# Projecting the queries of a pair of heads first: order q, k, k, q for k, k, q, q in two fused attention stages

## The reference

```python
x = x + attn_a(layernorm(x))   # q, k, v from x; 16 heads of 64; softmax(q k^T / (64*64*16)) v; WO
x = x + ffn(layernorm(x))      # gelu(x w1 + b1) w2 + b2, 256 -> 1024 -> 256
x = x + attn_b(layernorm(x))   # layernorm again, down to 128, up to q, k, v; RoPE on q and k; 1/sqrt(64)
x = x + ffn(layernorm(x))
```

## Time and profile before

| | before |
|---|---|
| median of 3 runs | 3870.42 us (3868.67 to 3873.36) |
| the profiled execution, its own time | 3868.46 us |
| its span | 3866.7 us |
| mean granted clock of TensorE, as a share of full speed | 0.978 |
| PE busy | 3650.3 us, 94% |
| POOL busy | 2624.3 us, 68% |
| PEld busy | 2354.9 us, 61% |
| DVE busy | 2262.3 us, 59% |
| ACT busy | 1689.1 us, 44% |
| DMA queue q1 (SP's) | 291.48 MB, 38.2% of 16 engines' span |

### The profile page before, as it was taken

One profiled execution on the slowest core, in us unless ns is written; L12 is line 12 of the kernel. 1 busy time (PEld: TensorE's weight loads), 2 busy tenths in 40 slices (PEclk: granted clock), 3 DMA queues, 4 the chain that ended last, 5 costly groups with the idle time before them and its releaser, 6 DMA issues. The chain is left out here.

```text
span 3866.7 us, 60118 instructions
## 1 busy us (share of the span) xinstructions
PE 3650.3 (94%) x16736; PEld 2354.9 (61%) x16736; DVE 2262.3 (59%) x2988; ACT 1689.1 (44%) x3212; POOL 2624.3 (68%) x1467
## 2 busy tenths in 40 slices
PE   3999999999999999997975999999999999999799
PEld 2566666666666666656863555555555555555488
DVE  5444444444444444445756777777777767777354
ACT  1344444444444444444542444444444444444354
POOL 2677777778777777773323777887788778777521
PEclk9999999999999999998996999999999999999899
DMA  6334433343344434421114455445544454554100
GB/s 194 81 80 88 103 78 75 84 109 84 81 85 87 95 75 86 87 47 32 44 62 90 80 86 103 83 84 86 103 83 84 83 105 82 85 83 83 40 17 28
DMA packets 419601, 313.68 MB, mean 81 GB/s; under 512 B 254753, under 2 KB 292513, under 8 KB 418465
## 3 DMA queue, kind: packets, MB, share of 16 engines
q1 hardware_dynamic: 414400, 291.48, 38.2%
q10 hardware_dynamic: 5088, 20.97, 1.5%
HBM read 88.35 MB, written 21.50 MB: 28 GB/s over the span
## 5 line engine op out<-in xcount | busy, mean ns | idle before, releaser
L887 POOL TENSOR_TENSOR a_rs<-a_rs,a_p 128x1024 f32<-128x1024 f32 x384 | 916.0, 2385 | 317.9 <-ACT a_p L797 301.0
L814 DVE TENSOR_REDUCE a_nmax<-a_ps_x 128x1 fp32r<-128x1024 f32 x512 | 627.2, 1225 | 759.4 <-PE a_ps_x L620 755.8
L887 POOL TENSOR_TENSOR b_rs<-b_rs,b_p 128x1024 f32<-128x1024 f32 x384 | 916.8, 2387 | 227.0 <-ACT b_p L797 208.9
L814 DVE TENSOR_REDUCE b_nmax<-b_ps_x 128x1 fp32r<-128x1024 f32 x512 | 626.7, 1224 | 326.5 <-PE b_ps_x L620 322.3
L797 ACT ACTIVATE a_p<-a_ps_s 128x512 f32<-128x512 f32 x1024 | 529.7, 607 | 413.6 <-PE a_ps_s L636 412.8
L797 ACT ACTIVATE b_p<-b_ps_s 128x512 f32<-128x512 f32 x1024 | 530.6, 608 | 340.6 <-PE b_ps_s L636 332.0
L652 PE MATMUL a_ps_o<-a_p,a_v 128*64 128x512 f32 x2048 | 467.7, 598 | 0.0
L652 PE MATMUL b_ps_o<-b_p,b_v 128*64 128x512 f32 x2048 | 467.7, 598 | 0.0
L635 PE MATMUL b_ps_s<-b_q,b_k 128*128 128x512 f32 x1024 | 419.5, 410 | 2.9 <-ACT b_p L797 1.5
L635 PE MATMUL a_ps_s<-a_q,a_k 128*128 128x512 f32 x1024 | 416.2, 406 | 3.0 <-DMA a_q<-a_nmax 3.0
L636 PE MATMUL b_ps_s<-b_q,b_k 128*128 128x512 f32 x1024 | 404.7, 395 | 0.0
(11 more groups left out here) (166 smaller groups left out, 5692.8 us busy)
## 6 DMA issues: line engine op xcount, KB each, us to landing
a_k<-a_nat_h SPq DMA_DIRECT2D x256, 128.0 KB, 2.4
a_q<-a_nat_h SPq DMA_DIRECT2D x256, 128.0 KB, 2.4
b_k<-b_nat_h SPq DMA_DIRECT2D x256, 128.0 KB, 3.9
b_q<-b_nat_h SPq DMA_DIRECT2D x256, 128.0 KB, 3.8
a_k<-a_nat_l SPq DMA_DIRECT2D x128, 128.0 KB, 2.4
a_q<-a_nat_l SPq DMA_DIRECT2D x128, 128.0 KB, 2.4
a_rinv<-rows_a SPq DMA_DIRECT2D x128, 128.0 KB, 3.0
b_k<-b_nat_l SPq DMA_DIRECT2D x128, 128.0 KB, 4.0
```

The source lines that it names most:

```text
L814: dve.reduce_max(nmax[:, g % 2, head, qi:qi + 1], ps_x[:].rearrange("p a b -> p (a b)"), AX_X, negate=True).then_inc(s_red, 1)
L887: pool.tensor_tensor(out, out, p[:, bb, i, :], ALU.add).then_inc(s_sum, 1)
```

## The change

In each pair the projections come as q of half 0, k of half 0, k of half 1, q of half 1. The same four projections are computed in the same places of PE's stream; what each of them is has changed. With it:

- `stack(4p)` is now a stack of q, whose slot is free early, so it moves to the top of the odd window; only `stack(4p + 1)`, k of half 0, stays at its end.
- `stack` and `convert` use buffer n % 2 as before; cosine, sine and feature columns go by the real half.
- q's split weights now serve n % 4 = 0 and 3, and live in two slots (`wq_h`, `wq_l` get a dimension of 2). Loads and splits of q and k swap places: wk in even windows, wq in odd ones.
- The lead-in loads and splits q's weights first.

The diff, cut to its core:

```diff
-        wq_r, wq_h, wq_l = sb("wq_r", [P, WC]), sb("wq_h", [P, WC], F32R), sb("wq_l", [P, WC], F32R)
+        wq_r, wq_h, wq_l = sb("wq_r", [P, WC]), sb("wq_h", [P, 2, WC], F32R), sb("wq_l", [P, 2, WC], F32R)
...
+        def which_half(n):
+
+            return ((1, 0), (0, 0), (0, 1), (1, 1))[n % 4]
...
         def maxima(pe, t, c):
...
-                        pe.wait_ge(s_stack[half], due(t, 2 * SD, SD * (pair + 1)))
-                pe.wait_ge(s_stack[2 + g % 2], due(t, 2 * SD, SD * (pair + 1)))
+                        pe.wait_ge(s_stack[1 + half], due(t, 2 * SD, SD * (pair + 1)))
+                pe.wait_ge(s_stack[3 * (g % 2)], due(t, 2 * SD, SD * (pair + 1)))
...
         def project_qk(pe, t, u, n):
...
+                pe.wait_ge(s_wq, due(t, 4, 2 * (pair + 1)))
+            if n % 4 == 1:
                 pe.wait_ge(s_wk, due(t, 4, 2 * (pair + 1)))
-            if n % 4 == 2:
-                pe.wait_ge(s_wq, due(t, 4, 2 * (pair + 1)))
...
         def pool_window(pool, t, u):
...
-                    split(pool, t, wk_r, wk_h, wk_l, s_wkr, s_unit, due(t, 8, 4 * pair - 2), s_wk, pair, 2)
+                    split(pool, t, wq_r, wq_h[:, pair % 2, :], wq_l[:, pair % 2, :], s_wqr, s_unit,
+                          due(t, 8, 4 * pair - 4), s_wq, pair, 2)
...
-                    split(pool, t, wq_r, wq_h, wq_l, s_wqr, s_unit, due(t, 8, 4 * pair), s_wq, pair, 2)
+                    split(pool, t, wk_r, wk_h[:], wk_l[:], s_wkr, s_unit, due(t, 8, 4 * pair - 1), s_wk, pair, 2)
...
         def sp_window(sp, t, u):
...
-            if u % 2 == 0 and live(t, 8, n, 4 * NPAIR):
+            if live(t, 8, n, 4 * NPAIR):
                 sp.wait_ge(s_nat_l, due(t, 8, n + 1))
                 stack(sp, n)
...
-            if u % 2 == 1 and live(t, 8, n, 4 * NPAIR):
-                stack(sp, n)
+            if u % 2 == 1 and live(t, 8, n + 1, 4 * NPAIR):
                 stack(sp, n + 1)
```

More of the change, by code:

```diff
@@ L684, in project_qk @@
         def project_qk(pe, t, u, n):
-            pair, which, half = n // 4, (n % 4) // 2, n % 2
+            pair = n // 4
+            which, half = which_half(n)
             if n % 4 == 0:
                 pe.wait_ge(s_feat, due(t, 16, 16 * (pair // 2 + 1)))
+                pe.wait_ge(s_wq, due(t, 4, 2 * (pair + 1)))
+            if n % 4 == 1:
                 pe.wait_ge(s_wk, due(t, 4, 2 * (pair + 1)))
-            if n % 4 == 2:
-                pe.wait_ge(s_wq, due(t, 4, 2 * (pair + 1)))
             pe.wait_ge(s_nat_l, due(t, 8, n))
-            w_h, w_l = (wk_h, wk_l) if which == 0 else (wq_h, wq_l)
+            w_h, w_l = (wk_h, wk_l) if which == 0 else (wq_h[:, pair % 2, :], wq_l[:, pair % 2, :])
             if rope is not None:
@@ L750, in convert_hi @@
         def convert_hi(act, t, n):
-            half, which = n % 2, (n % 4) // 2
+            half, which = n % 2, which_half(n)[0]
             if rope is None:
@@ L817, in rotate_odd @@
         def rotate_odd(dve, t, n):
-            cols = slice((n % 2) * BLOCK, (n % 2 + 1) * BLOCK)
+            half = which_half(n)[1]
+            cols = slice(half * BLOCK, (half + 1) * BLOCK)
             dve.wait_ge(s_unit, due(t, 8, n + 1))
@@ L907, in stack @@
         def stack(sp, n):
-            pair, which, half = n // 4, (n % 4) // 2, n % 2
+            pair = n // 4
+            which, half = which_half(n)
             for head in range(2):
                 rows = slice(D * head, D * (head + 1)) if rope is None else slice(head, P, 2)
-                hi, lo = nat_h[rows, half, :].bitcast(F32), nat_l[rows, half, :].bitcast(F32)
+                hi, lo = nat_h[rows, n % 2, :].bitcast(F32), nat_l[rows, n % 2, :].bitcast(F32)
                 if which == 0:
@@ L967, in sp_window @@
                 source = source_of(t, 3 + u // 2)
-                sp.wait_ge(s_wk, due(t, 4, u + 6))
-                sp.dma_start(wk_r[:], w_qk[source, :, WC:2 * WC]).then_inc(s_wkr, 16)
+                sp.wait_ge(s_wq, due(t, 4, u + 6))
+                sp.dma_start(wq_r[:], w_qk[source, :, 0:WC]).then_inc(s_wqr, 16)
             if u == 2 and live(t, 1, 2, BODIES):
@@ L1024, in _ @@
             pool.memset(q2[0:D, :, :, :].bitcast(F32), 0.0).then_inc(s_init, 1)
-            split(pool, 0, wk_r, wk_h, wk_l, s_wkr, s_unit, 0, s_wk, 0, 2)
+            split(pool, 0, wq_r, wq_h[:, 0, :], wq_l[:, 0, :], s_wqr, s_unit, 0, s_wq, 0, 2)
             pool.memset(ones[:], 1.0).then_inc(s_init, 1)
-            split(pool, -1, wv_r, wv_h, wv_l, s_wvr, s_vp, due(-1, 4, 4), s_wv, 1, 1)
+            split(pool, -1, wv_r, wv_h[:], wv_l[:], s_wvr, s_vp, due(-1, 4, 4), s_wv, 1, 1)
             run(pool, pool_window)
```

12 lines of the change are left out of this document (6 added, 6 removed).

## The result

The changed kernel takes 3847.40 us (median of 6 runs, 3845.88 to 3851.33); the kernel before, run between them, 3870.43. The ratio is 0.9943, with a 95% interval of 0.9932 to 0.9954: 23.0 us faster by the medians, where the sum said 24.1 and the forecast was 3846.

The account below looks back on a forecast made before the run. PE was taken as full in steady state, leaving lead-ins and transfer waits. Terms of 24.1 us took the profiled 3868.5 to 3844.4; against the median before, 3870.4, the forecast was 3846, range 3832 to 3860.

Parts of the forecast that it names:

- lead-in of a: Start of attention a: stack 0 goes once low part 0 is written, first maximum moves from 93.51 to about 89.7, -3.8 us.
- lead-in of b: Start of attention b: earlier stack 0 and no queue backlog move the first maximum from 2068.07 to 2064.0, -4.1 us.
- even windows of b: Steady state of b: ACT's wait for the stack of twelve ends, 0.22 us in 15 bodies, -3.3 us.
- reloads of b: Three feature reloads inside attention b: 3.5 of 6.7 us saved at each, -10.5 us, between -3 and -20.
- reloads of a: Three reloads in a: rinv issued earlier, next group's scores no longer wait 0.77 us for shift DMAs, -2.4 us.
- odd windows: Steady state: rinv's spread goes later, behind six stack DMAs, but POOL's multiply has 3.5 us of cover, cost 0.
- from there on the chain of maxima and reductions is what it was: Attention a after its first maximum: the chain is unchanged and starts earlier, keeping the 3.8 us.
- the first wait: Reload of b: PE's 1.53 us for the last stack DMA before the pair's first maximum goes or shrinks to half a microsecond.
- of 4.0 us idle about 2 stay: Each reload of b: PE's waits for the stack and for POOL's multiply behind rinv together shrink from 4.0 to about 2 us.
- A: Only the lead-ins move; PE idles as long at reloads because rinv still lands after them: 3858 us, chance 0.17.
- B: POOL's multiply in odd windows, behind stack and spread, becomes a bound: half a microsecond each, 3876.4 us, chance 0.04.
- C: Nothing gained: half-clock stretches swallow the lead-in shifts and steady state is PE's, 3866 us, chance 0.08.
- D: At reloads q1 keeps moving or rinv gets through, POOL's multiply is not late, stalls go whole: 3837 us, chance 0.16.

Follow-up runs that it names:

- the last kernel: Changed kernel with rinv ahead of the stack and b's reload halved, k and v's half behind window u=1's first exponential: 3835.83 us, ratio 0.9913.

## Why the prediction was right

The total was right, and the places and the kinds of the gains were right. Two sizes inside the largest term were not, and that the total came out within 1.1 us of the sum is in part luck. Term by term, with the values of the two profiles of the changed kernel:

| term | forecast | measured |
|---|---|---|
| lead-in of a | -3.8 | -2.9, -2.5 at the first maximum; -2.2, -2.2 at the first scores |
| lead-in of b | -4.1 | -4.1, -4.1 at both |
| even windows of b | -3.3 | -1.5 (23.46 to 23.34 us, 12 times without the reloads' own) |
| reloads of b | -10.5 | -4.4, -7.2 in the profiles, -8.2, -7.9 in the two others with these reloads; -9.7 by the medians without reloads |
| reloads of a | -2.4 | -3.0 (25.28, 25.24, 25.35 to 24.33, 24.29, 24.27) |
| odd windows | 0 | 0 (23.25 to 23.26 in b) |
| not in the sum: first body of b | | -1.1, -1.6 |

With 2.3 us for the lead-in of a (below) and 9.7 for the reloads of b these come to some 22 us, with the profiles' 7 to 8 for the reloads to some 20, for 23.0 measured. What fills the gap of 1 to 3 us was not found; the interval of the measurement is wider than that.

*Lead-in of a.* The shape was right, two sizes were not. The stack of projection 0 landed later than the 6.2 us I took from the earlier trace rows: the conversion of projection 2 starts at 82.49 for 81.9. A weight load now goes out just ahead of that stack (74.84, the stack at 75.38); whether it is the cause was not tried. SP's first issue of the next stack took 1.71 us instead of 0.64, so stack 2 went at 84.7 instead of 83.9. That 0.8 is about what the first maximum is short of (0.7). Then more is lost up to the first scores (24.29 us became 24.97, and 24.56 in the second profile), with a mean clock from 70 to 120 us of 0.76 in both profiles for 0.80 before. One execution says little here: in the eleven profiles of kernels that share this lead-in the first scores come 42.2 to 44.5 us behind the first projection, with a median of 44.0; the two kernels with the old one have 46.6 and 46.1. The kernel with only the early stack undone has 45.2, between them. So the lead-in of a is worth some 2.3 us. The steps that failed are the time of a stack's landing and "from there on the chain of maxima and reductions is what it was".

*Lead-in of b.* Right in every step, and the kernel with both lead-ins undone gives back 3.7 us of it.

*Even windows.* Mis-sized by a factor of two: of the 0.2 us between windows u=0 and u=1, 0.12 went, and the two are not equally long as I had said they would be. The wait of ACT that I named did vanish; a remainder near 0.1 us has another cause, and it stays even in the kernel without reloads. What it is was not tried. Against this, the same wait was larger in one place that the sum left out: in window u=2 of the first body of b, PE stood 0.96 us (its weight load 1.38) for exponentials behind a conversion that had waited 4.89 us for the twelve DMAs, and that window went from 25.68 to 24.57 us.

*Reloads of b.* The term is near by the medians (9.7 for 10.5) and too large by the profiles (4.4 to 8.2). Of the account, the events came as told: the first wait goes in ten of the twelve reloads of the four profiles (before that maximum 1.1 and 0.2 us are left in the other two, with no releaser named), rinv is still caught and leaves the second in all twelve, 1.3 to 2.6 us. The two-body stretch around the third reload was to take near 194 us: it takes 194.0 in the second profile and 196.1 in the first.

The step that failed is "of 4.0 us idle about 2 stay". That is 6 us less idle time in three reloads; the table at the changed kernel's repeat has 2.4 to 3.3 less (11.2 to between 7.9 and 8.8). The sum saw two waits and left out a third: the shifts stand behind rinv, and in ten of the twelve reloads the next window's first scores wait for one, 0.2 to 1.9 us. I had looked for that wait in a only.

The other part of the term was the half-clock stretch, of which I took half, some 4 us. I charged it as a fixed part of each reload; it comes or does not come. It costs 1.5 us and more at 4 of the twelve reloads, and 1.7 to 2.9 at five of the six reloads with the old order (the kernel before and the one with the steady state undone). With it the rest of the excess fell from 6.2 to between 0.5 and 4.9 us. So less than half of the gain at these reloads is idle time, in three of the four profiles, and more than half is the clock behind it. The clock gave back about what I took (1.3 to 5.7 us), the idle time half. That the total came out even so is in part luck: the first body of b and the reloads of a, which the sum had at nothing and at 2.4, gave some 2 us more than it said, and the medians have a further part that no profile shows.

*Reloads of a, odd windows.* Near the forecast (3.0 us for 2.4) and as forecast; the cover in odd windows is 5.1 us where I had bounded it at 3.5.

*The rivals.* A is refuted by the kernel with the steady state undone, B by the spread 5 us later that costs nothing measurable, C for b by the kernel with the lead-ins undone and for a by the eleven profiles. D said that rinv would get through the reload if q1 had a packet for each of q10's. The Trainium skill, in DMA: Bandwidth & Descriptors, section Queues, rings and completion order, has this rule. The trace agrees with it for a part of each reload only: 33 packets for 33 once q1 moves, but none of q1's for two microseconds and more before that. What I had taken for a weaker rule (62 packets for 110 in the earlier trace rows) fits such a start with equal turns behind it. The start, and the size of a reload's packet, keep rinv in the queue until the reload is nearly done. D's price, a reload without any stall, was there to be had, but by moving rinv and splitting the reload, not by this change.

## What to carry to other kernels

- Here a large transfer on a second queue held up the small DMAs in flight on the first for most of the time that it ran. Move such a transfer by what it would freeze: list the DMAs that someone waits for in the next microseconds, and put the large one behind the event that proves the last of them landed (here behind one exponential, 3 us later, which was worth 10 us). Splitting it without this moved the stall three times and removed it not once.
- Put first in a queue what the critical engine's helper needs soonest, rather than what is ready soonest: rinv before a stack was worth 6 us.
- When two profiles of one kernel differ by 3 us, price a term from several of them and with the cause cut out, by medians: one profile had this change's largest term at 4.4 us, three others at 7.2 to 8.2, the medians at 9.7.
- Split an excess into idle time and slower work before explaining it. Here most of what the reloads gave back was the half-clock stretch behind the wait, not the wait.

## What the runs showed that was not expected

- About a microsecond after its first packets a 2 MB load had the DMA engines to itself (47 packets of q10 and none of q1 from 2770 to 2772, with rinv in flight), and only from 2773 on did the two queues alternate, one packet each.
- Packets eight times smaller gave q1 more (rinv 7.4 us for 9.5 from issue to landing), and the load got slower by about as much as that was worth: two halves of 10.0 us, issued 0.8 us apart, for one of 9.6.
- Of two executions of one kernel with equal idle time at a reload (23.54 and 23.53 us busy in the window), one was followed by a stretch at 1.2 GHz and one was not. Where no idle time is left, as in the last kernel, none came: the granted clock is 1.00 in all six windows around its reloads.
